# Three sixteen-head attentions: side products spread over the slots, the mask of z moved ahead of the next score, and the normalise step moved to GpSimd

## The chip, the cores and the metric

The program runs on one core of one Trainium2 chip. The metric is the device time of the whole program in microseconds (us), the median of the runs shown.

## The reference

The program is a four-layer decoder on eight sequences of 256 tokens of 128 features. Twelve sublayers are added to the tokens `x` one after another, each on a layer norm of `x`. Three of them are attentions with sixteen heads of eight features, and only these are touched here:

```python
x = x + _L1_xattn_ref(_layernorm(x), ctx, ...)        # causal, then a two-layer MLP
x = x + _L2_xattn_ref(ctx, ctx, _layernorm(x), mask)  # keys and values from ctx, a given 0/1 mask
x = x + _L3_attn_ref(_layernorm(x), ...)              # causal, low-rank ("latent") weights
```

Each computes, for every head, softmax(q k^T * scale, masked) v over the 256 tokens of a sequence. The other nine sublayers are the same before and after.

## The kernel before

All three attentions are one function, `attention16`. A **unit** is one of the eight sequences; a **pair** is two of its sixteen heads, so there are 8 pairs in a unit and 64 in an attention. Tokens lie on the partitions in two halves of 128. An fp32 number is split into three bf16 pieces (GpSimd, `split_in_three`), and DMAs stack the pieces so that the six products of pieces are one bf16 matmul over 64 rows; two heads of a pair take rows 0 to 63 and 64 to 127 of the array.

The work is ordered by hand in **slots**, one pair a slot. Every engine walks the same slots and runs what falls due in each; semaphores join the engines. Pair n is scored in slot n. Twelve slots later (`BEHIND` = 12, and `r` is the slot less 12) its products are made again, transposed and with the row maxima subtracted, into the one buffer `ps_z`. In TensorE's order a slot is: `shift(r)` (z = scores again, transposed), `score(slot)`, `hide(ps_z)` (a matmul that adds the mask to z), `hide(ps_s)` (the same for the scores), `turn_back`, the side products, `weigh` (probabilities times values). Then:

- ScalarE takes exp of `ps_z` (L1667) when the hide of z is done; the next `shift` waits for that exp.
- VectorE reduces the scores to row maxima (`take_maxima`, L1354 and L1355, in the masked attention L1357). `ps_s` has two buffers, so a score waits for the maxima of two slots before.
- In even slots TensorE weighs four heads into `ps_o` (L1540). ScalarE copies the sums (L1673); in odd slots TensorE turns them back (L1555) and VectorE divides (`divide`, L1378 and L1382). `ps_o` is one bank, so a `weigh` waits for the `divide` before it.
- The **side products** share one bank, `ps_p`, each waiting until the one before is read out: maxima transposed (L1548), tokens transposed (L1469), q (L1475), k (L1479), v (L1486), the mixed heads transposed (mix, L1562), and in the masked attention the output projection (y, L1570). `xn`, the normalised tokens, is one buffer made on VectorE for the next unit (`normalise_unit`, L1342).
- After the maxima, VectorE splits them in three pieces (`split_maxima`) and SyncE stores them as rows of `queries` (L1266); the first `shift` of the unit, four slots later, waits for these rows.

By slot number modulo 8 the side products before are: 0 maxima, 2 mix and tokens, 3 y and q, 4 k, 6 v. The first attention has no y in the slots (an MLP follows) and the latent one has neither mix nor y: it adds to `x` from `mixed` in position 3.

An attention begins with slots before pair 0, in which unit 0 and 1 are prepared. TensorE runs three 512-column filler matmuls (L54) in each negative slot, and twelve in slot 0. GpSimd sets up constants, splits q and k, turns the integer masks into bf16 (`make_masks`) and adds the output bias (`add_bias`).

## Time and profile before

| what | value |
|---|---|
| median of 3 runs | 1993.07 us (1988.14 to 1995.74) |
| span of the profiled execution | 1991.5 us |
| TensorE busy | 1615.1 us, 81% |
| VectorE busy | 1231.2 us, 62% |
| ScalarE busy | 823.4 us, 41% |
| GpSimd busy | 606.1 us, 30% |
| first, masked, latent attention: first shift to last shift | 112.6, 163.2, 111.0 us |

The span runs from the first to the last instruction of one profiled execution; it lies 1.6 us below the median. The profile gives no time of its own for that execution besides the span. In the tables PE is TensorE's matmuls, PEld its weight loads, DVE is VectorE, ACT ScalarE, POOL GpSimd. The profile leaves the digits off the tile names, so `x_` is the first as well as the masked attention, and `a_` is the latent one.

### The profile page before, as it was taken

The page shows a single profiled execution, that of the slowest core. Times are in us where ns is not written, and L with a number is a line of the kernel's source. Part 1 is how long each engine was busy: PE and PEld are TensorE (multiplying, and loading weights), DVE is VectorE, ACT ScalarE, POOL GpSimd, SP SyncE. Part 2 cuts the span into 40 slices and gives each one's busy share as a digit, 9 for nine tenths or more (in the row PEclk, how much of TensorE's full clock was granted, in tenths as well). Part 3 has the DMA queues.
Part 4 walks back from the last instruction along what each step waited for, and adds up shares of the span by engine and source line. Part 5 has one row for each costly group of instructions (what it writes and reads, how often), then busy time and mean ns, then how long its engine had stood idle before and what let it go on. Part 6 is the DMA issues. An engine that isn't in the chain of part 4 may idle for free. (4 is left out here: it accounts for less than half of the span.)

```text
span 1991.5 us, 34855 instructions
## 1 busy us (share of the span) xinstructions
PE 1615.1 (81%) x12400; PEld 1077.5 (54%) x12400; DVE 1231.2 (62%) x4249; ACT 823.4 (41%) x1760; POOL 606.1 (30%) x742
## 2 busy tenths in 40 slices
PE   3378767888779897757988799978877888999888
PEld 1146434454547787644444366745546654677556
DVE  6868645575378999533666333326848875899632
ACT  2232345366227786732344443314643410333422
POOL 4605122430024535304531000022202115777221
PEclk8677877999879999878999898889988987999999
DMA  2000001320036777613321000022210000000000
GB/s 86 0 12 1 10 30 50 83 60 14 7 128 213 262 248 262 219 37 116 84 58 38 18 1 0 1 61 65 62 61 3 1 0 1 2 2 3 2 0 22
DMA packets 81332, 115.59 MB, mean 58 GB/s; under 512 B 8464, under 2 KB 62608, under 8 KB 80400
## 3 DMA queue, kind: packets, MB, share of 16 engines
q0 software_dynamic: 18432, 67.38, 9.7%
q1 hardware_dynamic: 60144, 44.90, 8.1%
q8 instruction: 96, 1.57, 0.3%
q10 hardware_dynamic: 2592, 1.18, 0.3%
q14 instruction: 68, 0.56, 0.1%
HBM read 88.85 MB, written 1.05 MB: 45 GB/s over the span
## 5 line engine op out<-in xcount | busy, mean ns | idle before, releaser
L2643 POOL DMA_INDIRECT f_rows<-tree_table,f_index x128 | 128.8, 1006 | 185.8 <-DVE f_index L2704 75.7
L2844 PE MATMUL f_ps_y<-f_rows,shared_sb 128*128 128x128 f32 x1024 | 129.2, 289 | 31.3 <-ACT f_rows L2916 31.3
L2916 ACT ACTIVATE f_rows<-f_rows,f_low_act 128x128 f32<-128x128 f32 x512 | 153.0, 387 | 0.8
L1667 ACT ACTIVATE x_probs<-x_ps_z 128x768 f32<-128x768 f32 (+1 forms) x128 | 117.4, 917 | 85.6 <-PE x_ps_z L1527 57.6
L82 POOL TENSOR_TENSOR rstd<-moments,shared_sb 128x12 f32<-128x12 f32 (+3 forms) x22 | 4.6, 207 | 480.9 <-DVE moments L66 480.8
L2844 PEld LDWEIGHTS f_ps_y<-f_rows,shared_sb 128*128 128x128 f32 x1024 | 124.5, 203 | 37.2 <-ACT f_rows L2916 33.9
L2743 DVE CUSTOM_DVE_ANT_0 f_rows<-f_rows,f_xn 128x128 f32<-128x128 f32 x512 | 111.3, 287 | 24.2 <-DMA f_rows<-tree_table,f_index 24.2
L1357 DVE TENSOR_REDUCE x_minus_max<-x_ps_s 128x4 f32<-128x1024 f32 x64 | 77.8, 1223 | 73.7 <-PE x_ps_s L1527 73.5
L2095 PE MATMUL f_ps_h<-f_xnT,weights 128*128 128x512 f32 x144 | 76.7, 661 | 2.4 <-ACT f_hT L2160 2.1
L2160 ACT ACTIVATE f_hT<-f_ps_h,weights 128x512 f32<-128x512 f32 x72 | 48.6, 685 | 71.4 <-PE f_ps_h L2095 69.7
L2072 DVE SCALAR_TENSOR_TENSOR x_tokens<-f_ps_y,f_chosen,x_tokens 128x128 f32 (+1 forms) x128 | 36.0, 344 | 67.1 <-PE f_ps_y L2107 67.1
L2107 PEld LDWEIGHTS f_ps_y<-weights,f_hT 128*128 128x128 f32 x576 | 69.7, 192 | 14.3 <-issue 12.6
L3382 ACT ACTIVATE r_probs<-r_ps_z 128x768 f32<-128x768 f32 x64 | 51.9, 810 | 58.5 <-PE r_ps_z L3262 58.5
L2107 PE MATMUL f_ps_y<-weights,f_hT 128*128 128x128 f32 x576 | 73.2, 278 | 0.0
L1514 PE MATMUL x_ps_z<-x_queries,x_keys 64*128 64x256 bf16 (+1 forms) x512 | 46.8, 261 | 27.0 <-ACT x_probs L1667 25.8
L3064 POOL TENSOR_TENSOR r_q_swapped<-r_q_swapped,weights 128x256 f32<-128x256 f32 x64 | 58.4, 912 | 31.4 <-DVE r_q_swapped L3118 30.8
L1540 PE MATMUL x_ps_o<-x_probs,x_v_ones 128*32 128x256 f32 (+1 forms) x1024 | 61.7, 358 | 2.0 <-DVE x_mixed L1382 1.2
L1667 ACT ACTIVATE a_probs<-a_ps_z 128x768 f32<-128x768 f32 x64 | 51.8, 810 | 27.3 <-PE a_ps_z L1523 27.2
L3262 PE MATMUL r_ps_z<-r_queries,r_keys 64*128 64x256 f32 (+1 forms) x512 | 59.1, 350 | 2.8 <-ACT r_probs L3382 2.7
L3250 PE MATMUL r_ps_s<-r_keys,r_queries 64*128 64x128 f32 (+1 forms) x512 | 54.0, 329 | 4.1 <-DVE r_minus_max L3127 2.6
L2836 PE MATMUL f_ps_y<-weights,f_maskedT 128*128 128x128 f32 (+2 forms) x384 | 54.2, 292 | 3.3 <-ACT f_maskedT L2903 3.3
L3262 PEld LDWEIGHTS r_ps_z<-r_queries,r_keys 64*128 64x128 f32 x512 | 44.1, 186 | 21.8 <-issue 14.1
(661 smaller groups left out, 4191.6 us busy)
## 6 DMA issues: line engine op xcount, KB each, us to landing
x_queries<-x_pieces SPq DMA_DIRECT2D x96, 64.0 KB, 2.1
x_keys<-x_pieces SPq DMA_DIRECT2D x84, 64.0 KB, 2.1
a_queries<-a_pieces SPq DMA_DIRECT2D x48, 64.0 KB, 2.1
weights<-w_L_ffn SPq DMA_DIRECT2D x1, 2953.5 KB, 9.9
a_keys<-a_pieces SPq DMA_DIRECT2D x42, 64.0 KB, 2.1
weights<-w_L_ffn SPq DMA_DIRECT2D x1, 2449.0 KB, 9.7
weights<-w_L_ffn SPq DMA_DIRECT2D x1, 2176.0 KB, 9.2
f_rows<-tree_table,f_index POOLq DMA_INDIRECT x128, 6.1
```

The lines of the kernel that those rows point to most:

```text
L1357: last = v.tensor_reduce(peaks.rearrange("p j h -> p h j"), scores.rearrange("p h (j k) -> p h j k", j=HALVES), AX.X, ALU.max, negate=True)
L1540: last = pe.matmul(out[V1 * i:V1 * (i + 1), a:T], v_ones[:, u % KEPT, half, SIDE * group + i, :], probs[:, r % HELD, i % 2, at:at + T - a] ...
L1667: a.activation(probs[:, r % HELD, :, :], ps_z[:, :, 0:WIDE], ACT.Exp, scale=scale).then_inc(exped, 1)
L2095: pe.matmul(ps_h[:, i % 2, :], w["up"][:, i * P:(i + 1) * P], xnT[:, :], start=True, stop=True).then_inc(up_made, 1)
L2107: last = pe.matmul(out, hT[:, i % 4, j * P:(j + 1) * P], w["down"][:, i * P:(i + 1) * P], start=c == 0, stop=c == CH - 1 and e < E)
L2643: pool.indirect_dma_start(rows[:, place(u, j), tree, :], None, g.tree_table, bass.IndirectOffsetOnAxis(index[:, u % 2, low, j * TREES + tr ...
L2743: last = v.tensor_tensor_reduce(row, row, xn[:, u % KEPT, j, :], 1.0, 0.0, ALU.mult, ALU.add, low_act[:, u % 3, j * TREES + tree, f:f + 1])
L2836: last = pe.matmul(ps_y[:, u % SUMS, j, :], maskedT[0:k, i, :], w["out"][0:k, i * P:(i + 1) * P], start=j == 0 and i == 0, stop=False)
L2844: last = pe.matmul(ps_y[:, u % SUMS, j, :], g.ident, rows[:, place(u, j), tree, OUT + f * D:OUT + (f + 1) * D], start=False, stop=(low, j, ...
L2916: last = a.activation(row, row, ACT.Copy, scale=low_act[:, u % 3, j * TREES + tree, f:f + 1])
L3064: step(pool.tensor_tensor(part, part, w["sin_q"], ALU.mult))
L3262: last = pe.matmul(ps_z[:, i, out], keys[rows, u % RINGS, k:k + P], queries[rows, u % RINGS, p, q:T], start=q == 0, stop=q > 0)
```

## The change

Three edits, all in `attention16`:

1. The slots of the side products move. By slot number modulo 8 they are afterwards: 0 maxima, 1 y, 2 tokens, 3 q, 4 mix, 5 k, 7 v; position 6 has none. The latent attention's add moves from position 3 to 4. The normalise step of a unit moves from 15 to 18 slots ahead of its first score, and with it the load of the masks on SyncE's queue. The slots now begin three earlier, at -18 for -15, and end two later.
2. On TensorE the hide of z stands directly behind `shift`, ahead of the next `score`.
3. All units but the first are normalised on GpSimd instead of VectorE. In GpSimd's order the step comes ahead of the slot's bias, splits and masks.

```diff
--- before.py
+++ after.py
@@ -1160,7 +1160,7 @@
     GROUPS = NH // SIDE
     LAG = 4
     BEHIND = PAIRS + LAG
-    FIRST, LAST = -PAIRS - 7, ALL + BEHIND + PAIRS + 4
+    FIRST, LAST = -PAIRS - 10, ALL + BEHIND + PAIRS + 6
     RINGS, HELD, KEPT = 4, 4, 4
     STACK_DMAS = 2 * len(PRODUCTS) + 1
     SEEN = ((slice(0, P), slice(STACK, P)), (slice(0, STACK), slice(0, P)))
@@ -1209,12 +1209,12 @@
 
         unit_at = lambda n: n // PAIRS if n % PAIRS == 0 and 0 <= n < ALL else None
         pair_at = lambda n: n if 0 <= n < ALL else None
-        norm_in, tokens_in, q_in, k_in, v_in = (lambda slot, early=e: unit_at(slot + early) for e in (15, 14, 13, 12, 10))
+        norm_in, tokens_in, q_in, k_in, v_in = (lambda slot, early=e: unit_at(slot + early) for e in (18, 14, 13, 11, 9))
         queries_out, keys_out = (lambda slot, early=e: unit_at(slot + early) for e in (11, 8))
         maxima_in = lambda slot: unit_at(slot - PAIRS)
         group_in = lambda r, late: (r - late) // 2 if r % 2 == late % 2 and 0 <= (r - late) // 2 < ALL // 2 else None
         weighed_in, sums_in, back_in = (lambda r, late=n: group_in(r, late) for n in (2, 3, 5))
-        mix_in, y_in = (lambda r, late=n: unit_at(r - late) for n in (14, 15))
+        mix_in, y_in = (lambda r, late=n: unit_at(r - late) for n in (16, 21 if tail else 16))
         slots = range(FIRST, LAST)
 
         side_taken = {"maxima": maxima_taken, "mix": mix_taken, "y": y_taken, "tokens": tokens_taken, "q": q_taken, "k": k_taken, "v": v_taken}
@@ -1320,7 +1320,17 @@
                 pool.tensor_tensor(g.x[:, of, :], g.x[:, of, :], w["out_b"].rearrange("p (o d) -> p o d", o=1).broadcast_to([P, HALVES, D]),
                                    ALU.add).then_inc(bias_added, 1)
 
+            def normalise_unit(u):
+                pool.wait_ge(xT_made, u)
+                for half in range(HALVES):
+                    n = u * HALVES + half
+                    last = pool.tensor_scalar(xn[:, half, :], g.x[:, n, :], g.moments[:, n, 0:1], g.rstd[:, n:n + 1],
+                                              ALU.subtract, ALU.mult)
+                last.then_inc(xn_ready, 1)
+
             for slot in slots:
+                if norm_in(slot) is not None and norm_in(slot) > 0:
+                    normalise_unit(norm_in(slot))
                 if tail and v_in(slot - 1) is not None:
                     add_bias(v_in(slot - 1))
                 if q_in(slot) is not None:
@@ -1335,11 +1345,9 @@
         def _(v):
             step = Chain(v, steps)
 
-            def normalise_unit(u):
-                v.wait_ge(xT_made, u)
+            def normalise_first():
                 for half in range(HALVES):
-                    n = u * HALVES + half
-                    last = v.tensor_scalar(xn[:, half, :], g.x[:, n, :], g.moments[:, n, 0:1], g.rstd[:, n:n + 1],
+                    last = v.tensor_scalar(xn[:, half, :], g.x[:, half, :], g.moments[:, half, 0:1], g.rstd[:, half:half + 1],
                                            ALU.subtract, ALU.mult)
                 last.then_inc(xn_ready, 1)
 
@@ -1402,7 +1410,7 @@
                     last = v.bn_stats(g.x_stats[:, n, :], g.x[:, n, :])
                 last.then_inc(stats_taken, 1)
 
-            normalise_unit(0)
+            normalise_first()
             v.wait_ge(g.loaded[name], 16)
             if causal:
                 by_half = lambda m: w[m].rearrange("p (i k) -> p i k", i=2)
@@ -1415,8 +1423,6 @@
             v.memset(v_ones[:, :, :, :, :], 1.0).then_inc(ones_ready, 1)
             for slot in slots:
                 r = slot - BEHIND
-                if norm_in(slot) is not None and norm_in(slot) > 0:
-                    normalise_unit(norm_in(slot))
                 if pair_at(slot) is not None:
                     take_maxima(slot)
                 if maxima_in(slot) is not None:
@@ -1581,12 +1587,11 @@
                     fill_wait(pe, g, ps_z[:, 0, :], 512, 5)
                 if pair_at(r) is not None:
                     shift(r)
+                    hide(ps_z, r // PAIRS, 1).then_inc(shifted, 1)
                 if pair_at(slot) is not None:
                     score(slot)
                 if not causal and unit_at(slot) is not None:
                     pe.wait_ge(mask_ready, unit_at(slot) + 1)
-                if pair_at(r) is not None:
-                    hide(ps_z, r // PAIRS, 1).then_inc(shifted, 1)
                 if pair_at(slot) is not None:
                     hide(ps_s[:, slot % 2, :, :], slot // PAIRS, 0).then_inc(scored, 1)
                 if back_in(r) is not None:
```

## Rows read from the trace of the kernel before

**Rows 1.** Windows view, masked attention, slots 12 to 75 (busy us by engine)
```profile
962.80:1126.00 163.20, 141.85 (x1345) 69.11 (x1345) 91.06 (x174) 84.19 (x118) 42.11 (x49) 1.00 0.18 46
```

**Rows 2.** Timeline, latent attention, slots 53 to 55 (start, duration, engine, line)
```profile
1441.82 0.34 PE L1514 MATMUL a_ps_z<-a_queries,a_keys 64*128 64x256 bf16 x4
...
1442.70 0.43 DVE L1354 TENSOR_REDUCE a_minus_max<-a_ps_s 128x2 f32<-128x256 f32 x1
...
1443.40 0.34 PE L1514 MATMUL a_ps_z<-a_queries,a_keys 64*128 64x256 bf16 x4 [0.38 <-ACT a_probs L1667]
...
1444.16 0.59 PEld L1540 LDWEIGHTS a_ps_o<-a_probs,a_v_ones 128*32 128x32 f32 x16 [0.16 <-DVE a_mixed L1382]
...
1444.97 0.34 PE L1514 MATMUL a_ps_z<-a_queries,a_keys 64*128 64x256 bf16 x4
```

**Rows 3.** Timeline, first attention: starts of slots 32, 33, 35, 36 and 40
```profile
417.62 0.34 PE L1514 MATMUL x_ps_z<-x_queries,x_keys 64*128 64x256 bf16 x4 [0.37 <-ACT x_probs L1667]
...
419.49 0.34 PE L1514 MATMUL x_ps_z<-x_queries,x_keys 64*128 64x256 bf16 x4
...
424.16 0.34 PE L1514 MATMUL x_ps_z<-x_queries,x_keys 64*128 64x256 bf16 x4
...
425.83 0.34 PE L1514 MATMUL x_ps_z<-x_queries,x_keys 64*128 64x256 bf16 x4
...
433.36 0.34 PE L1514 MATMUL x_ps_z<-x_queries,x_keys 64*128 64x256 bf16 x4 [0.38 <-ACT x_probs L1667]
```

**Rows 4.** Timeline, latent attention: starts of slots 40, 48, 52 and 56
```profile
1417.73 0.34 PE L1514 MATMUL a_ps_z<-a_queries,a_keys 64*128 64x256 bf16 x4 [0.37 <-ACT a_probs L1667]
...
1433.01 0.34 PE L1514 MATMUL a_ps_z<-a_queries,a_keys 64*128 64x256 bf16 x4 [0.37 <-ACT a_probs L1667]
...
1440.25 0.34 PE L1514 MATMUL a_ps_z<-a_queries,a_keys 64*128 64x256 bf16 x4 [0.46 <-ACT a_probs L1667]
...
1446.55 0.34 PE L1514 MATMUL a_ps_z<-a_queries,a_keys 64*128 64x256 bf16 x4 [0.37 <-ACT a_probs L1667]
```

**Rows 5.** Timeline, masked attention: starts of slots 32, 40, 51, 52 and 53
```profile
1016.61 0.39 PE L1514 MATMUL x_ps_z<-x_queries,x_keys 64*128 64x256 bf16 x4 [0.47 <-ACT x_probs L1667]
...
1040.32 0.39 PE L1514 MATMUL x_ps_z<-x_queries,x_keys 64*128 64x256 bf16 x4 [0.47 <-ACT x_probs L1667]
...
1071.74 0.39 PE L1514 MATMUL x_ps_z<-x_queries,x_keys 64*128 64x256 bf16 x4
...
1074.09 0.40 PE L1514 MATMUL x_ps_z<-x_queries,x_keys 64*128 64x256 bf16 x4
...
1076.61 0.39 PE L1514 MATMUL x_ps_z<-x_queries,x_keys 64*128 64x256 bf16 x4
```

**Rows 6.** Timeline, masked attention: an exp after the last score
```profile
1124.87 1.02 ACT L1667 ACTIVATE x_probs<-x_ps_z 128x1024 f32<-128x1024 f32 x1 [1.02 <-PE x_ps_z L1527]
```

**Rows 7.** Timeline, masked attention: matmuls that change the row count on TensorE
```profile
952.64 1.24 PE L54 MATMUL x_ps_z<-filler 128*128 128x512 bf16 x5
...
953.81 0.39 PE L1502 MATMUL x_ps_s<-x_keys,x_queries 64*128 64x256 bf16 x4
...
1098.74 0.38 PE L1502 MATMUL x_ps_s<-x_keys,x_queries 64*128 64x256 bf16 x4
...
1099.05 0.61 PE L1527 MATMUL x_ps_z<-x_masks,x_ident 128*128 128x512 bf16 x2
```

**Rows 8.** Timeline, latent attention: its first fillers and first token transposes
```profile
1323.94 2.72 PE L54 MATMUL a_ps_s<-filler 128*128 128x512 bf16 x6 [1.06 <-PEq L1735]
...
1326.45 0.64 PE L1469 MATMUL a_ps_p<-shared_sb,a_xn 128*128 128x128 f32 x2
```

**Rows 9.** Timeline (first row) and views of lines L92 and L3053 (ns min/median/max)
```profile
1405.80 0.58 DVE L1342 TENSOR_SCALAR a_xn<-x_tokens,moments,rstd 128x128 f32<-128x128 f32 x2
...
L92 POOL TENSOR_SCALAR a_xn<-x_tokens,moments,rstd x12: 784/2026/2768, 25.7 to 74.6; 128x128 f32<-128x128 f32 x12
...
L3053 POOL TENSOR_SCALAR f_hid<-x_tokens,moments,rstd x16: 787/794/1299, 1680.1 to 1844.2; 128x128 f32<-128x128 f32 x16
```

## The prediction

> **What bounds the kernel now.** I read the windows view first, for the slots in which both halves of the pipeline run, then the timeline slot by slot. In the masked attention TensorE is busy 141.85 of 163.20 us at full clock, VectorE 91 and GpSimd 42 [rows 1]. TensorE is near its limit, yet not at it, so a slot's length has to be read. A slot is the distance from one `shift` (L1514) to the next. "Position" below is the slot number modulo 8.
>
> The light slots of the causal attentions (no side product) show two chains of the same length. Slot 53 starts at 1441.82 and slot 54 at 1443.40, which waited 0.38 us for the exp: 1.58 us for shift, score, hide of z and exp. But the pair of slots ends only at 1444.97, and there the other chain ends too: scores hidden, reduce at 1442.70, divide, and `weigh` at 1444.16, which had waited 0.16 us for VectorE's `mixed`; the next shift follows 0.81 us later [rows 2]. So an odd and an even slot together take 3.15 us by VectorE's chain alone. An earlier exp cannot shorten that.
>
> A full unit (eight slots with all sides) takes 433.36 - 417.62 = 15.74 us in the first attention [rows 3], 1433.01 - 1417.73 = 15.28 us in the latent one, and a light unit 13.54 us. In the light unit positions 0 to 3 take 1440.25 - 1433.01 = 7.24 us and positions 4 to 7 take 6.30 us [rows 4]. The first four hold the split of the maxima on VectorE and the rows that its DMAs store. In the masked attention a full unit takes 23.71 us [rows 5].
>
> **Edit 1 and 3, causal attentions.** Positions 0 to 3: VectorE's chain and the stored rows gave 7.24 us in the light unit, where nothing was normalised and only maxima stood beside. With the normalise gone from VectorE (0.58 us, two instructions [rows 9]) and mix gone from position 2, a full unit should come down to the same 7.24 us: tokens hide under the wait of `weigh`. Positions 4 to 7: an even slot with two transposes takes 419.49 - 417.62 = 1.87 us, an odd slot with q takes 425.83 - 424.16 = 1.67 us [rows 3]; a plain even slot takes 1.57 us [rows 2]. So the first attention gets 1.87 (mix) + 1.67 (k) + 1.57 + 1.67 (v) = 6.78, a unit of 14.02 us, 1.72 less. In the latent one position 4 is plain, but the add now stands on VectorE between the maxima of positions 4 and 5, where it was behind the divide. The light slots show 3.24 us in place of 3.15 where the add is near [rows 4]; here I charge 0.4 us, for the add and statistics less VectorE's idle time: 1.57 + 1.67 + 1.88 + 1.67 = 6.79, a unit of 14.03 us, 1.25 less. There are three full units in each (slots 24 to 47). The unit before them, without mix or add, saves 1.56, and slots 12 to 15 about 0.9 (k and v leave slots that weigh or start to). The two light units lose a little: mix stands in the open now, +0.13 each in the first, and the late add costs +0.23 each in the latent one. Sum: first 3 x 1.72 + 1.56 + 0.9 - 0.26 = 7.4 us, latent 3 x 1.25 + 1.56 + 0.9 - 0.46 = 5.8 us.
>
> In slots 0 to 11 no exp runs and VectorE's reductions set the pace, so each normalise that leaves it (0.58 us, twice) shortens them by something between nothing and itself: 0.8 us in each causal attention, 1.3 in the masked one (its scores are longer and one of its two normalises runs beside a busy GpSimd). Together 2.9.
>
> **Edit 2.** In the causal attentions every matmul of shift, score and hide uses 64 rows, so the exchange costs TensorE nothing. It brings the exp forward by the time of a score, and [rows 2] say that this is worth nothing in a light pair. I take 0; the bound on the other side is half of the exp wait of 0.38 us in some 20 odd slots of each, 7 us in both.
>
> In the masked attention the hides use all 128 rows and the score 64. Before, a slot had the order 64, 64, 128, 128; afterwards 64, 128, 64, 128: two more changes. A score's four matmuls of 256 columns, two at a time, are issued in 0.21 us, but the hide follows 0.31 us after its start; and behind five fillers (5 x 0.21 us = 1.05, a filler being half of the 0.42 us that it takes at half clock [rows 8]) the 64-row score starts after 1.17 us [rows 7]. So each change costs about 0.10 us, and each slot that TensorE bounds gets 0.20 us longer. The exp alone would allow 2.04 us a slot (1.02 idle and 1.02 of its own, with no score between [rows 6]).
>
> The Trainium skill, "TensorEngine Tiling (Array Packing)", Key Properties, says that a change of tiling mode, not just of tile, drains TensorE. By that rule this edit has a price; the trace agrees with a gap at each change. A full drain read as the 0.19 us by which five modelled fillers outlast their issue (1.24 for 1.05) would make the slot 0.38 longer rather than 0.20, 8 us more in all.
>
> With 0.20 the slots of the masked attention are: even plain 2.52 + 0.20 = 2.72; even with two transposes 2.93 (0.21 more, my estimate, between 0 and the 0.30 of [rows 3]); odd with y, q, k or v 2.35 + 0.20 = 2.55; odd plain 2.1, an estimate at which TensorE's own work and the exp come out alike [rows 5, 6]. A full unit is 3 x 2.93 + 2.72 + 4 x 2.55 = 21.7 us. The waits of position 2 (tokens for mix) and 3 (q for VectorE's add) are gone, since each side's reader has a slot's time. That saves 2.0 us in each of two full units and 2.3 in the third before y begins. The first unit loses 0.5, the two light ones 0.45 each (four even slots and y pay 0.20, three plain odd ones win 0.18), slots 12 to 15 win 0.45. Sum: 5.4 us.
>
> **The three early slots.** Each attention begins 9 fillers later: its six took 1326.45 - 1323.94 = 2.51 us at half clock before the first transposes [rows 8], so nine are 3.8 us, and 1.9 at full clock. TensorE has nothing else to do then, and everything behind waits: q, its split, the keys' DMAs on ScalarE's queue. Part comes back because the clock has risen by the time the projections run, where it was at half in part, and because the first split no longer runs beside VectorE's long memset. I take 1.8, 2.2 and 1.2 us, 5.2 in all; bounds 0 and 11.4.
>
> **GpSimd.** A normalise is two tensor_scalar of 128x128. GpSimd shows 0.79 us in the median for this form in one stage and 2.03 (0.78 to 2.77) in another, beside heavy VectorE work [rows 9]. At 0.79 a unit costs 1.6 us, at 2.77 5.5. It falls due at position 6 and is needed by the tokens at position 2, four slots on, never under 5.6 us; GpSimd is three quarters idle [rows 1]. I take 0: the cover is that idle time; without it one late unit costs up to 4 us. The masks load earlier on SyncE and are needed 18 slots on: 0. The last unit's output in the masked attention has one add more in line ahead of mix: +1, by judgment, since y of the unit before now comes after the last divide.
>
> **Sum.** -7.4 - 5.8 - 5.4 - 2.9 + 5.2 + 1.0 = -15.3, say -15. The span of 1991.5 becomes 1976.5; it stands 1.6 under the median, so the median of 1993.07 becomes 1978.
>
> **The rivals.**
> - *The exchange is worth its face.* Row changes cost nothing under the longer streams, and the causal light pairs do shorten. The masked attention then gains 9 us more (about 45 slots x 0.20) and the causal ones up to 7. For it: exp waits stand in front of nearly every odd slot's end. Against it: the gaps of [rows 7] and the 0.16 us of [rows 2]. Time: 1978 - 9 - 3 (half of the 7) = 1966. Chance 0.14.
> - *Given back.* The waits move instead of going: the longer lead-in costs its 3.8 us in full three times (+6), and tokens or k meet a late GpSimd or a late reader in the full units (+0.5 us in ten units). Time: 1978 + 11 = 1989, not to be told from no change. For it: one shared bank and one `xn` leave every side behind the one before. Against it: the slack that the spread leaves by [rows 3 to 5]. Chance 0.29.
> - *Slower: the row changes cost more than they did*, because the hide of z and the weight loads of the score can't overlap and the weight queue runs dry. Place: the masked attention's 52 scoring slots. Each slot would need 0.7 us for two changes in place of 0.20 to make the whole slower by 0.5% (15 + 10 = 25 us over 52 slots, 0.5 each). At 0.8 the time is 1978 + 31 = 2009. For it: it is the one edit with a price in every slot. Against it: the two changes that are read cost 0.10 to 0.12 each [rows 7]. Chance 0.07.
> - The forecast itself: 0.50.
>
> **Chances and range.** One can tell from no change only what is over about 0.5%, 10 us. Faster 0.50 + 0.14, of which a little falls inside 10 us: 0.62. Same: 0.31. Slower: 0.07. The range reaches down to the first rival and up to the second, 1965 to 1989; the forecast's own is 1970 to 1986.
>
> **What would show it.** Windows over the three stretches should be 105, 158 and 105 us from first to last shift. A full unit should be 14.0, 21.7 and 14.0 us. No tokens or q wait for ScalarE's mixT or VectorE's add. The masked attention's slots should show the hide 0.31 us behind the shift and the score 0.3 behind the last hide's issue. Light causal units should not be shorter. POOL's new rows should be near 0.8 us each, with tokens never waiting on them past slot 0. The first score of each attention should come 1 to 2.5 us later than before, counted from its first filler. The forecast is wrong if light pairs shorten (chain misread), if tokens wait on GpSimd, or if a masked slot grows by other than 0.2.

## The result and the profile after

The changed kernel takes 1959.87 us (median of 4 runs, 1956.94 to 1962.79) against 1990.69 us for the kernel before (4 runs): ratio 0.984, 95% interval 0.982 to 0.986. The forecast was 1978 with a range of 1965 to 1989; it has the right sign, the gain is twice what it said, and the time lies below the range. A second measurement of the same kernel later gave 1962.60 against 1989.99 us, ratio 0.986 (0.984 to 0.988).

The table splits the span of each profile at the same events: the first filler of an attention, its first score, the first and the last shift (slots 12 and 75), and the first instructions of the stages between. The starts are read to 0.1 us, that of the last shift at its fourth matmul, so these stretches are 0.1 us longer than the distance from shift to shift ([rows 1] and the windows below). "Untouched" is all the rest, whose code is the same in both kernels (but for the last slots of the first attention, which are counted there).

| us | before | after | change | forecast |
|---|---|---|---|---|
| first filler to first score, three attentions | 23.6, 23.4, 24.8 | 23.1, 23.7, 22.9 | -2.1 | +5.2 |
| slots 0 to 11 | 16.2, 20.0, 16.2 | 16.5, 19.1, 15.9 | -0.9 | -2.9 |
| slots 12 to 75, first attention | 112.7 | 103.8 | -8.9 | -7.4 |
| slots 12 to 75, masked | 163.3 | 155.7 | -7.6 | -5.4 |
| slots 12 to 75, latent | 111.1 | 104.2 | -6.9 | -5.8 |
| tails of masked and latent | 13.4, 10.0 | 14.9, 10.4 | +1.9 | +1.0 |
| sum | 534.7 | 510.2 | -24.5 | -15.3 |
| untouched | 1456.8 | 1444.8 | -12.0 | 0 |

The windows view of the changed kernel over slots 12 to 75 of the first, the masked and the latent attention, the middle one answering to [rows 1] (columns: stretch, length, busy us and count of PE, PEld, DVE, ACT, POOL, then granted clock, DMA share, GB/s):

```profile
375.20:478.90 103.70, 94.48 (x1549) 59.45 (x1550) 72.45 (x190) 71.80 (x118) 30.62 (x52) 1.00 0.20 48
943.40:1099.00 155.60, 146.88 (x1320) 59.54 (x1344) 89.38 (x166) 85.94 (x118) 48.60 (x57) 1.00 0.18 45
1337.20:1441.30 104.10, 92.58 (x1535) 58.18 (x1534) 77.44 (x218) 70.38 (x113) 27.50 (x47) 1.00 0.20 47
```

In the masked attention TensorE's busy time rose from 141.85 to 146.88 us while the stretch shrank by 7.6: it now leaves 9 us idle. The rise belongs to the exchange: the changed kernel without it (an experiment below) is busy for 137.94 us of 151.30. The timeline of the masked attention's slot 54 and the start of slot 55 shows where it comes in (start, duration, engine, line; rows of VectorE and most weight loads are left out, here and in the timelines below):

```profile
1051.17 0.39 PE L1520 MATMUL x_ps_z<-x_queries,x_keys 64*128 64x256 bf16 x4
1051.49 0.60 PE L1533 MATMUL x_ps_z<-x_masks,x_ident 128*128 128x512 bf16 x2
1052.03 0.12 PEld L1508 LDWEIGHTS x_ps_s<-x_keys,x_queries 64*128 64x128 bf16 x4 [0.42 <-issue]
1052.03 0.39 PE L1508 MATMUL x_ps_s<-x_keys,x_queries 64*128 64x256 bf16 x4
1052.14 1.02 ACT L1672 ACTIVATE x_probs<-x_ps_z 128x1024 f32<-128x1024 f32 x1 [1.02 <-PE x_ps_z L1533]
...
1052.36 0.60 PE L1533 MATMUL x_ps_s<-x_masks,x_ident 128*128 128x512 bf16 x2
1052.89 1.07 PE L1546 MATMUL x_ps_o<-x_probs,x_v_ones 128*32 128x256 f32 x16
...
1053.90 0.39 PE L1520 MATMUL x_ps_z<-x_queries,x_keys 64*128 64x256 bf16 x4
```

A shift or score is issued in 0.21 us and two hides in 0.42. Start to start here: shift to hide 0.32, hide to score 0.54, score to hide 0.33, hide to `weigh` 0.53: every one is 0.11 to 0.12 us longer than its issue. The score's first weight load starts together with its first matmul here; in slot 53 of the kernel before, where the score follows a shift of the same tile, it started 0.11 us ahead of it (1076.73 for 1076.84). Whether the price of a change is a drain of the array or this load that nothing hides, no run separates. The exp starts 0.97 us after the shift, where it started 1.2 us after it. The slot is 2.73 us.

The starts of the first attention's slots 33, 34, 35 and 41 in the timeline, to be set beside [rows 3]:

```profile
410.02 0.34 PE L1520 MATMUL x_ps_z<-x_queries,x_keys 64*128 64x256 bf16 x4
...
411.43 0.34 PE L1520 MATMUL x_ps_z<-x_queries,x_keys 64*128 64x256 bf16 x4 [0.21 <-ACT x_probs L1672]
...
413.73 0.34 PE L1520 MATMUL x_ps_z<-x_queries,x_keys 64*128 64x256 bf16 x4
...
423.80 0.34 PE L1520 MATMUL x_ps_z<-x_queries,x_keys 64*128 64x256 bf16 x4
```

A full unit, here from slot 33 to slot 41, is 13.78 us (15.74 before, 14.02 forecast). GpSimd's normalise, in the view of its line:

```profile
L1327 POOL TENSOR_SCALAR x_xn<-x_tokens,moments,rstd x28: 783/792/806, 347.4 to 1013.6; 128x128 f32<-128x128 f32 x28
L1327 POOL TENSOR_SCALAR a_xn<-x_tokens,moments,rstd x14: 790/792/804, 1310.1 to 1384.3; 128x128 f32<-128x128 f32 x14
...
  PE x_ps_p L1475: 3.2, 2
  PE a_ps_p L1475: 1.6, 1
```

It is 0.79 us each time, as assumed, and TensorE's tokens waited for it three times, once in each lead-in.

### The profile page after: what moved, and what is told of

Same layout as the page of the kernel before. It is cut to its first block and busy times, and to the rows that moved or that the text cites. A ratio compares the mean times of both kernels' runs of the same rounds, so it can differ in the third digit from the quotient of the medians.

```text
span 1955.0 us, 34849 instructions
## 1 busy us (share of the span) xinstructions
PE 1599.1 (82%) x12367; PEld 1058.0 (54%) x12427; DVE 1219.7 (62%) x4207; ACT 824.3 (42%) x1760; POOL 638.0 (33%) x784
## 5 line engine op out<-in xcount | busy, mean ns | idle before, releaser
L2165 ACT ACTIVATE f_hT<-f_ps_h,weights 128x512 f32<-128x512 f32 x72 | 48.6, 685 | 71.8 <-PE f_ps_h L2100 70.0
L1672 ACT ACTIVATE a_probs<-a_ps_z 128x768 f32<-128x768 f32 x64 | 51.9, 810 | 13.4 <-PE a_ps_z L1529 12.4
```

The costliest lines, as they stand in the source:

```text
L1672: a.activation(probs[:, r % HELD, :, :], ps_z[:, :, 0:WIDE], ACT.Exp, scale=scale).then_inc(exped, 1)
```

## The experiments

All times are of slots 12 to 75 unless another stretch is named, in the order first, masked, latent; before they are 112.7, 163.3, 111.1 and after 103.8, 155.7, 104.2 us. Whole-kernel ratios are to the kernel before, with their 95% intervals. Within one kernel a given slot repeats to 0.01 or 0.02 us from unit to unit, and slots 12 to 75 repeat to 0.4 us from one profile to the next, which is why most verdicts rest on slots and not on medians. Stretches outside them do not repeat so well.

### The kernel before once more

> The kernel before once more, with nothing changed. It measures what a comparison here can tell and how much a stage that no edit touches differs from one execution to the next. In the traces of before and after the untouched stages together differ by about 11 us (4.7 us ahead of the first attention, 4.0 in the trees, 2.5 in the block behind the latent attention), the touched ones by about 24. Theory A (scatter): the ratio is 1.000 within 0.3%, and the first filler of the first attention starts between 335 and 340 us, the stage from 534.2 to 919.4 lasts 381 to 386 us. Theory B (the untouched stages are shorter in the changed kernel for a reason of the change, such as the place of its code): the untouched stages repeat the times of before within 1 us in all, 339.9 us and 385.2 us.

Ratio 0.9996 (0.9979 to 1.0013); the 19 runs of before in this batch lay between 1987.3 and 2000.1 us. Slots 12 to 75: 112.7, 163.3, 111.5. The stretch before the first attention took 338.9 us and the trees (a long untouched stage between the first attention and the masked one) 382.9, for 339.9 and 385.2: scatter, as the first theory had it. First filler to first score, the **lead-in** from here on, took 24.5, 23.0, 23.4, so a single lead-in differs by up to 1.4 us in the same kernel (and by 3.7 in the changed kernel's repetition below).

### Edit 1 alone: side products in slots of their own

```diff
-  FIRST, LAST = -PAIRS - 7, ALL + BEHIND + PAIRS + 4
+  FIRST, LAST = -PAIRS - 7, ALL + BEHIND + PAIRS + 6
...
-  norm_in, tokens_in, q_in, k_in, v_in = (... (15, 14, 13, 12, 10))
+  norm_in, tokens_in, q_in, k_in, v_in = (... (15, 14, 13, 11, 9))
...
-  mix_in, y_in = (... (14, 15))
+  mix_in, y_in = (... (16, 21 if tail else 16))
```

> Edit 1 alone: side products in slots of their own, the normalise step still on VectorE 15 slots ahead, hide of z behind the score, no early slots. Forecast on record: it is this edit that gains; the masked attention without the price of the row changes gets some 14 us shorter from slot 12 to 75 (5.4 + 9), the first 7, the latent 5.5: about -26 us in all, a full masked unit 20.9 to 21.0 us. Rival (the exchange carries part of the gain and costs TensorE nothing): masked -6 to -8, first and latent -6 and -4, about -17 in all, a full masked unit 21.5 us or more.

Ratio 0.988 (0.985 to 0.990). Slots: 107.5, 151.6, 107.6, so -5.2, -11.7, -3.5. A full masked unit is 19.86 to 20.41 us. The spread is the largest gain, and nearest to the forecast (-7, -14, -5.5) in the masked attention. In full units of the causal ones position 2 takes 2.64 us (before: 3.10 in the first, 2.64 in the latent), because VectorE's normalise still holds its place there: with the normalise on GpSimd and all else alike it is 2.13 (the changed kernel without edit 2, below).

### Edit 2 alone: hide of z behind the shift

```diff
     if pair_at(r) is not None:
         shift(r)
+        hide(ps_z, r // PAIRS, 1).then_inc(shifted, 1)
     if pair_at(slot) is not None:
         score(slot)
...
-    if pair_at(r) is not None:
-        hide(ps_z, r // PAIRS, 1).then_inc(shifted, 1)
```

> Edit 2 alone: the hide of z directly behind the shift in all three attentions. Forecast on record: nothing in the causal attentions (light unit 13.54 us), and 0.20 us more in each TensorE-bound slot of the masked one, about 45 of them: +9 us in all. Rival (worth its face): the causal attentions lose their waits for the exp, 0.38 us in 20 odd slots each, -7 us together, and the masked one pays 0.20 in even slots only and wins it back in odd ones: 0 to -3; total -7 to -10.

Ratio 0.996 (0.994 to 0.998). Slots: 109.1, 164.5, 108.8, so -3.6, +1.2, -2.3. In the causal attentions the odd slots of positions 1, 5 and 7 fall from 1.58 to 1.41 us and position 3 with q from 1.67 to 1.57; the even ones with k or v stay at 2.18 to 2.20, and a light unit falls from 13.54 to 13.22 in the first attention and to 13.31 in the latent one. In the masked attention an even slot goes from 2.52 to 2.73 and an odd one from 2.26 to 2.05. The forecast that [rows 2] make the exp worthless is refuted: the exp bounded the odd slots, and with its wait cut from 0.38 to 0.21 us the first attention's light pairs of positions 4 to 7 take 3.03 and 3.11 us, not 3.15.

### Edit 3 alone: normalise on GpSimd

```diff
-  FIRST, LAST = -PAIRS - 7, ...
+  FIRST, LAST = -PAIRS - 10, ...
...
-  norm_in, ... (15, 14, 13, 12, 10)     # called on VectorE
+  norm_in, ... (18, 14, 13, 12, 10)     # called on GpSimd, unit 0 on VectorE
```

> Edit 3 alone: all units but the first normalised on GpSimd, 18 slots ahead, three early slots with nine more fillers, sides and hides as before. Forecast on record: lead-ins +5.2 us together, slots 0 to 11 -2.9, and in full units VectorE is relieved of 1.16 us at a place where the tokens, not VectorE, are late (mix in the same slot), so 0 to -0.5 a unit, -4 at most: total -2 to +2. Rival (the lead-in costs nothing, because the nine fillers lift the clock before the projections): lead-ins 0 to -1, total -3 to -6.

Ratio 0.993 (0.990 to 0.995). Slots: 112.3, 163.4, 109.2. Where tokens do not share their slot with mix, position 2 falls from 2.64 to 2.13 us; where they do (first and masked, full units) nothing moves. Slots 0 to 11 take 16.2, 19.0, 15.6, and the lead-ins 23.2, 23.8, 23.5. The touched stretches give -5.0 us, where -2 to +2 had been expected and -3 to -6 by the rival; the ratio's interval begins at -9. The rest of it is not in them (the untouched code took 1449.4 us in this profile, 7.4 less than in that of the kernel before), and it is not explained by this run.

### Nine more fillers and nothing else

```diff
-  FIRST, LAST = -PAIRS - 7, ...
+  FIRST, LAST = -PAIRS - 10, ...
```

> The kernel before with three empty slots more at the start of each attention, so nine more fillers of 512 columns and nothing else. It prices the lead-in. Forecast on record: +1.9 to +3.8 us a lead-in less what the risen clock gives back, 1.2 to 2.2 each, +5.2 in all. Rival (TensorE has slack in the lead-in: before, it sat idle 3.86 us there until ScalarE had copied the second unit's tokens): the first filler to the first score lasts 23 to 24.5 us as before in each, 0 in all.

Ratio 1.000 (0.998 to 1.002). Lead-ins 24.7, 25.4, 25.3 us: 3.6 us more than before in all, 4.5 more than in its repetition. So the fillers alone cost a good part of the 5.2 us forecast, and in the changed kernel something gives it back. Against edit 3 alone, which has the same fillers, the lead-ins are 1.5, 1.6 and 1.8 us longer. The timeline of the first attention's second unit says where. First the kernel before, then edit 3 alone; the bracket is TensorE's idle time and what ended it:

```profile
355.39 1.19 PE L1475 MATMUL x_ps_p<-x_xnT,weights 128*128 128x256 f32 x2 [3.86 <-ACT x_xnT L1645]
```

```profile
349.39 0.41 PE L1475 MATMUL x_ps_p<-shared_sb,x_xn 128*128 128x128 f32 x2 [1.44 <-POOL x_xn L1327]
...
352.25 0.67 PE L1481 MATMUL x_ps_p<-x_xnT,weights 128*128 128x256 f32 x2 [1.81 <-ACT x_xnT L1651]
...
353.49 0.70 PE L1485 MATMUL x_ps_p<-x_xnT,weights 128*128 128x256 f32 x2
```

Before, TensorE had run out of fillers and stood still for 3.86 us in one piece, until ScalarE had issued the first unit's key DMAs and copied the second unit's tokens; behind it q took 1.19 us and k 0.98, near twice their 0.67 and 0.59 us at full clock. With fillers alone the gap is 3.45 us and k takes 1.06 behind it. With the normalise on GpSimd the tokens come later, the gap falls in two parts of 1.44 and 1.81 us, and q and k take 0.67 and 0.70 at full clock. The changed kernel has 1.61 and 1.81 us there, and the same 0.67. The mean granted clock of that lead-in is 0.82 before, 0.86 with fillers alone and 0.92 with edit 3 alone and in the changed kernel. Behind the gap of 3.86 us the granted clock was 0.50 (1.2 GHz), behind the split one 1.00 (2.4 GHz).

### The changed kernel without edit 2

```diff
     if pair_at(r) is not None:
         shift(r)
-        hide(ps_z, r // PAIRS, 1).then_inc(shifted, 1)
     if pair_at(slot) is not None:
         score(slot)
...
+    if pair_at(r) is not None:
+        hide(ps_z, r // PAIRS, 1).then_inc(shifted, 1)
```

> The changed kernel with edit 2 undone in all three attentions. From the runs of single edits (slots 12 to 75, change against before in us): sides -5.2, -11.7, -3.5; exchange -3.6, +1.2, -2.3; GpSimd -0.4, +0.1, -1.9; all three together -8.9, -7.6, -6.9. New theory: the exchange is worth what the exp-bound slots can give. In the causal attentions odd slots go from 1.58 to 1.41 us while they carry no side, and are 1.57 either way with one; in the masked one odd slots go from 2.26 to 2.05 without a side but are 2.38 for 2.26 with one, and even slots pay 0.21. So without the exchange slots 12 to 75 should last about 105.5, 150.7 and 105.7 us (after: 103.8, 155.7, 104.2), -1.8 in all against the changed kernel. Rival (gains add up): 107.4, 154.5, 106.5, +4.7.

Ratio 0.987 (0.983 to 0.991). Slots: 105.4, 151.3, 105.3. So inside the changed kernel edit 2 is worth -1.6, +4.4, -1.1: together it costs 1.7 us, where alone it gained 4.7. The timeline of slot 45 of the masked attention (odd, with k) in the kernel without edit 2 shows why:

```profile
1031.11 0.39 PE L1520 MATMUL x_ps_z<-x_queries,x_keys 64*128 64x256 bf16 x4
...
1031.34 0.38 PE L1508 MATMUL x_ps_s<-x_keys,x_queries 64*128 64x256 bf16 x4
1031.65 0.60 PE L1533 MATMUL x_ps_z<-x_masks,x_ident 128*128 128x512 bf16 x2
...
1032.30 1.02 ACT L1673 ACTIVATE x_probs<-x_ps_z 128x1024 f32<-128x1024 f32 x1 [0.67 <-PE x_ps_z L1533]
1032.53 0.38 PE L1561 MATMUL x_ps_o<-shared_sb,x_sumsT 128*128 128x128 f32 x2
...
1032.75 0.60 PE L1485 MATMUL x_ps_p<-ctx_features,weights 128*128 128x256 f32 x2
1033.37 0.39 PE L1520 MATMUL x_ps_z<-x_queries,x_keys 64*128 64x256 bf16 x4
```

The exp ends at 1033.32 and k at 1033.35: the slot of 2.26 us is full on both sides. Bringing the exp forward then gives nothing, and two more changes make it 2.38. In the kernel before, k and v stood in even slots and the exp alone bounded every odd slot but position 3 of the full units.

### Edit 2 in the causal attentions only

```diff
+    if pair_at(r) is not None and causal:
         hide(ps_z, r // PAIRS, 1).then_inc(shifted, 1)
...
+    if pair_at(r) is not None and not causal:
+        hide(ps_z, r // PAIRS, 1).then_inc(shifted, 1)
```

> The changed kernel with edit 2 undone in the masked attention alone. New theory: 103.8, 150.7 and 104.2 us from slot 12 to 75, 5 us less than the changed kernel, a full masked unit 19.9 us for 21.1. Rival (the exchange alone cost the masked attention 1.2 us, and that is what it costs here): 1.2 us less, 154.5 us.

Ratio 0.987 (0.984 to 0.990), median 1963.80. Slots: 103.8, 151.3, 104.2: the masked stage is 4.4 us shorter than in the changed kernel, as expected, while the median shows none of it. Its other stages took 1452.5 us.

### The changed kernel without edit 3

```diff
-  FIRST, LAST = -PAIRS - 10, ...
+  FIRST, LAST = -PAIRS - 7, ...
...
-  norm_in, ... (18, 14, 13, 11, 9)      # called on GpSimd
+  norm_in, ... (15, 14, 13, 11, 9)      # called on VectorE
```

> Edits 1 and 2 without edit 3: normalise on VectorE 15 slots ahead, no early slots. If VectorE's normalise stands in the way of the tokens once mix has left their slot, position 2 is 2.8 us for 2.29 in four units of each causal attention: slots 12 to 75 last 105.9, 156.7 and 106.3 us, +5 in all against the changed kernel. Rival (GpSimd is worth only what it was alone, 0.4 and 1.9): 104.2, 155.6, 106.1, +2.2. Either way the lead-ins are within 1 us of 23.6.

Ratio 0.989 (0.987 to 0.992). Slots: 105.9, 156.0, 106.0. Edit 3 is worth 2.1 and 1.8 us in the causal attentions (position 2: 2.80 against 2.30), five times what it was worth alone in the first, and 0.3 in the masked one. The lead-ins are 24.5, 23.1 and 24.2 us, 71.8 in all as in the kernel before.

### The changed kernel once more

> The changed kernel once more. The stages that no edit touches took 1444.8 us in its first profile, and between 1449.4 and 1465.6 us in nine other kernels with the same code there, at granted clocks that differ. Theory A (the first profile met a high clock in them; the change itself is worth the 24.5 us of the touched stages): the touched stages repeat within 1 us (slots 12 to 75 103.8, 155.7, 104.2 us), the untouched ones take 1450 us or more, and the ratio is nearer 0.987 than 0.984. Theory B (the change shortens the untouched stages too): they take 1447 us or less again and the ratio is 0.984 or lower.

Theory A holds for the slots (103.8, 155.7, 104.2), the untouched stages (1453.7 us) and the ratio (0.986). It does not hold for the lead-ins: they took 23.0, 23.1 and 26.6 us, so the touched stretches are 22.1 us shorter than before in this profile, not 24.5. The latent lead-in has the same two gaps as the first profile, but the granted clock fell in it and q took 1.19 us. Here is q's timeline row, then the windows of the latent lead-in in the first profile and in this one:

```profile
1317.78 1.19 PE L1481 MATMUL a_ps_p<-a_xnT,a_w_q 128*128 128x256 f32 x2 [1.74 <-ACT a_xnT L1650]
...
1298.40:1321.20 22.80, 19.37 (x84) 9.48 (x84) 5.15 (x8) 3.42 (x8) 11.68 (x22) 0.92 0.51 140
...
1300.50:1327.10 26.60, 23.18 (x86) 10.87 (x88) 5.11 (x7) 3.43 (x8) 12.58 (x23) 0.77 0.49 131
```

Over all fourteen profiles the untouched code took 1444.8 to 1465.6 us. The windows view shows what goes with it, first the stretch before the first attention and that behind the latent one in the changed kernel's first profile, then the same two stretches of the kernel of the next experiment, whose untouched code took 1465.1 us:

```profile
0.00:335.60 335.60, 204.07 (x942) 126.22 (x952) 223.06 (x524) 115.91 (x196) 109.91 (x109) 0.77 0.06 20
...
1451.80:1955.00 503.20, 435.88 (x3278) 306.21 (x3294) 342.94 (x1085) 152.60 (x342) 198.95 (x254) 0.93 0.03 10
```

```profile
0.00:343.70 343.70, 212.87 (x943) 136.05 (x953) 223.18 (x524) 116.00 (x196) 109.93 (x109) 0.75 0.06 20
...
1460.90:1970.00 509.10, 440.78 (x3278) 308.12 (x3294) 343.73 (x1085) 152.75 (x342) 198.41 (x254) 0.92 0.03 9
```

VectorE, ScalarE and GpSimd are busy for the same time within 0.5%; TensorE alone is busy for longer, 8.8 and 4.9 us, at a mean granted clock of 0.75 for 0.77, and 0.92 for 0.93.

### Three repairs, the first on the number of changes

```diff
+    if not causal:          # in score(r), ahead of its matmuls
+        for i in range(2):
+            pe.matmul(ps_s[...], ident16, masks[...], start=True, stop=False)
...
-  mix_in, y_in = (... (16, 21 if tail else 16))
+  mix_in, y_in = (... (16, 21 if tail else 15))
-    if slot < 0:
+    if -PAIRS - 7 <= slot < 0:
         fill_wait(pe, g, ps_s[:, 0, 0, :], 512, 3)
```

> The changed kernel with three repairs, in stages that do not touch each other. (a) Masked attention: on TensorE shift, hide of z, hide of s, score, so the exp stays early and the row count changes twice a slot instead of four times. New theory (each change costs 0.10 us): even slots go back from 2.72 to 2.52 and 2.94 to 2.73, odd slots stay at 2.05 without a side and take 2.20 with one; slots 12 to 75 last 143 to 146 us for 155.7. Rival (it is the hide of z between shift and score that costs, not the number of changes): 155 us as now, or 151 as without the exchange. (b) Latent attention: the add one slot earlier, behind the maxima of position 3; position 6 goes from 2.07 to 1.55 us in full units and from 2.00 to 1.70 in light ones, slots 12 to 75 last 102 us for 104.2. (c) No fillers in the three early slots: the first filler to the first score 22 us for 23.1, 23.7, 22.9 if the fillers delay the first tokens and the clock rises anyway, no less if the clock then falls in the wait for the second unit.

Ratio 0.986 (0.984 to 0.988). Slots: 103.8, 155.7, 102.9. (b) held in direction: -1.3 us, position 6 at 1.79 us for 2.07. Position 6 had been expected at 1.55, and the stretch at 102. (c) held: lead-ins 22.4, 22.8, 22.0, 2.5 us less in all than in the changed kernel's first profile, although the granted clock fell in each. The next two kernels drop the fillers too, and there it is 1.9 and 0.6 less. (a) failed as forecast: even slots 2.62 plain, 2.99 with tokens or mix, odd slots with a side 2.42, where 2.52, 2.73 and 2.20 had been expected. My count had left out two places: hide or score to `weigh` is a change as well (128 to 32 columns), and a score that stands last needs one more before the turn back. Counted so, a plain even slot has three changes from shift to weigh (after: four; before: two), and the three lengths 2.62, 2.73, 2.52 differ by 0.10 a change.

### Score at the end of the slot

```diff
     shift(r)
     hide(ps_z, ...)
-    score(slot)             # masks first, then scores
+    mask_scores(slot)       # the masks alone, start=True
     turn_back, side products, weigh
+    score(slot)             # masked attention only
```

> As the last kernel, but in the masked attention the score stands at the end of TensorE's slot, directly ahead of the next shift; hide of s still directly behind hide of z. Read from the starts in the run before: every change of the matmul's tile costs 0.10 to 0.12 us over the issue of 0.21 us, that between hide or score and weigh (128x128 or 64x128 to 128x32) as well, so moving the score behind the hides had not taken two changes away: four of them stand in an odd slot and in one with transposes, three in a plain even one (2.42, 2.99, 2.62 us measured). New theory (0.10 for each change, wherever it stands): now score and next shift share a tile, one change fewer in plain even slots and two fewer in the others: even plain 2.52, even with two transposes 2.73 to 2.79, odd with a side 2.20, odd plain 2.04 by the exp; slots 12 to 75 last 146 to 148 us (changed kernel 155.7, without the exchange 151.3). Rival (what costs is that the hide of z stands directly behind the shift, not the changes): even slots stay at 2.62 and 2.99, 155 us. The other stages as in the run before: 103.8 and 102.9 us, first filler to first shift 38.3, 41.8 and 37.9 us. The ratio: 9 us less than the changed kernel in the masked attention and some 5 in the rest, 0.979 to 0.984.

Ratio 0.989 (0.986 to 0.992). Slots: 103.9, 162.4, 103.0. The forecast of 146 to 148 us failed. Odd slots with a side came down to 2.17 us, but `weigh` now waits for VectorE, as in slot 36:

```profile
1013.14 1.07 PE L1559 MATMUL x_ps_o<-x_probs,x_v_ones 128*32 128x256 f32 x16 [0.29 <-DVE x_mixed L1390]
```

### VectorE's maxima at the end of its slot, too

```diff
-    if pair_at(slot) is not None:
+    if causal and pair_at(slot) is not None:
         take_maxima(slot)
     ...  # split, divide, add
+    if not causal and pair_at(slot) is not None:
+        take_maxima(slot)
```

> As the last kernel, with VectorE's order changed to match in the masked attention: split, divide and add ahead of the slot's maxima. The last kernel bore out the price of the changes on TensorE (odd slots with a side 2.17 us for 2.42, and 2.80 for 2.99 in the even one with mix once its wait is taken off), but lost more: the score now ends the slot, its maxima start behind it, and the divide stood behind them, so each weigh waited 0.29 to 0.90 us for VectorE's mixed, y 0.68 us for the split, tokens 0.83 us for the add. Theory: these waits go. Even plain 2.52, even with tokens or mix 2.80, with maxima 2.75 to 2.95 (it needs the maxima of the last score, which end 1.4 us after that slot), odd with a side 2.17, odd plain 2.04; slots 12 to 75 last 147 to 149 us, against 155.7 in the changed kernel and 151.3 without the exchange. Rival (the maxima, 1.23 us of each slot, are late whatever the order, because they cannot start before the slot's end): weigh still waits and the stage lasts 155 us or more.

Median 1955.78 us (5 runs) against 1991.32, ratio 0.982 (0.979 to 0.984). Slots: 103.9, 148.9, 102.8: the shortest masked attention of all, 14.4 us under before. Slot 54 in the timeline, beside that of the changed kernel above:

```profile
1048.87 0.39 PE L1535 MATMUL x_ps_z<-x_queries,x_keys 64*128 64x256 bf16 x4
1049.19 0.61 PE L1548 MATMUL x_ps_z<-x_masks,x_ident 128*128 128x512 bf16 x2
1049.63 0.59 PE L1523 MATMUL x_ps_s<-x_masks,x_ident 128*128 128x512 bf16 x2
1049.83 1.02 ACT L1687 ACTIVATE x_probs<-x_ps_z 128x1024 f32<-128x1024 f32 x1 [1.02 <-PE x_ps_z L1548]
1050.16 1.07 PE L1561 MATMUL x_ps_o<-x_probs,x_v_ones 128*32 128x256 f32 x16
1051.16 0.39 PE L1510 MATMUL x_ps_s<-x_keys,x_queries 64*128 64x256 bf16 x4
...
1051.39 0.38 PE L1535 MATMUL x_ps_z<-x_queries,x_keys 64*128 64x256 bf16 x4
```

Two changes fewer, 2.52 us for 2.73, and the exp starts just as early after the shift. Score and next shift follow each other in 0.23 us. Even slots with mix are 2.73, odd ones with a side 2.17, odd plain ones 2.04. Only position 0 pays, 3.12 us for 2.94, since it waits 0.23 us for the maxima of the score just ahead. The forecast of 147 to 149 us held.

## Why the prediction was wrong

What failed most is the term for the three early slots: nine fillers, with "everything behind waits", were to cost 5.2 us, and the lead-ins came out 2.1 us shorter (0.9 longer in the second profile). Next to it stand the step that called the earlier exp worthless in light pairs, and the price of 2.55 us for an odd masked slot with a side. The gains of edit 1 and of the normalise were forecast well, and no rival of the three describes the outcome. The first one, the exchange worth its face, is nearest in time (1966) but its mechanism is half wrong: the exchange costs time in the changed kernel. Step by step:

- **Sides and normalise in the causal attentions: right.** -7.4 and -5.8 us had been forecast with nothing for the exchange; the changed kernel without the exchange shows -7.3 and -5.8, full units of 13.90 and 13.93 us (14.02 and 14.03) and 7.24 us in positions 0 to 3 (7.24). In this the near-exact sums are in part luck, since small errors cancel: odd slots with k or v are 1.58 us, not 1.67, and the light units of the first attention lost 0.36 us each instead of 0.13. The 1.67 was read in position 3, which takes 1.67 us in light units too, where the first attention has no side in it; nor is the 3.24 us of positions 3 and 4 the add's doing, as the first attention has the same without an add. The add is charged at 0.4 us but stands in the sum at 0.31 (1.88 for 1.57); it measured 0.38 without the exchange and 0.50 in the changed kernel.
- **"An earlier exp cannot shorten that": wrong.** The step took VectorE's 3.15 us for the pair's limit, but both chains ended together in [rows 2]: the exp of slot 54 ends at 1444.92 us, 0.05 us ahead of the next shift, as the row that stands between them shows.

```profile
1444.11 0.81 ACT L1667 ACTIVATE a_probs<-a_ps_z 128x768 f32<-128x768 f32 x1 [0.77 <-PE a_ps_z L1523]
```

  Moved alone, the exp gives 0.32 us a light unit in the first attention, and 0.17 us in positions 1, 5 and 7 and 0.10 in position 3 of a full one. In the changed kernel that is -1.6 and -1.1 us.
- **Row changes at 0.10 each: right.** The even slots grew by 0.21, from 2.52 to 2.73 and from 2.73 to 2.94, where 0.20 had been forecast for each. The Trainium skill, "TensorEngine Tiling (Array Packing)", Key Properties, says that a change of tiling mode drains TensorE. In kind the traces agree: every change has a price, here 0.10 to 0.12 us. The prediction's reading of a drain as 0.19 us each would have made these slots 2.90 and 3.11, and that is refuted. **"Odd with y, q, k or v 2.35 + 0.20 = 2.55": the term that was mis-sized.** It measured 2.38. The 2.35 was read in slot 51, position 3; other odd slots were at 2.26. Both stood there because of the exp, not of TensorE's work, so two changes on TensorE took the place of a wait. In slots 16 to 47 fourteen odd slots hold a side (y only from slot 33 on), which makes 14 x 0.17 = 2.4 us, about the 2.2 by which the masked stage beat the forecast. What else differs nearly cancels (slots 64 to 75, for which nothing was charged, take 0.34 us more).
- **The lead-ins: the largest error.** +5.2 forecast, -2.1 measured (and +0.9 in the second profile, whose latent lead-in took 26.6 us). The fillers alone cost 3.6 to 4.5 us, not far from it. The step "everything behind waits" overlooked the 3.86 us for which TensorE stood still ahead of the second unit, and what went with it on the clock. Edit 3 breaks that wait in two and took 1.5 to 1.8 us back in each attention. All 42 lead-ins of the fourteen profiles, by what stood in them:

| second unit normalised on | nine fillers more | TensorE's idle time, us | clock fell in or behind it | mean lead-in, us |
|---|---|---|---|---|
| VectorE | no | one gap, 3.2 to 4.6 | 15 of 15 | 23.9 |
| VectorE | yes | one gap, 3.3 to 3.5 | 3 of 3 | 25.1 |
| GpSimd | yes | two gaps, 1.4 to 1.6 and 1.7 to 1.8 | 1 of 15 | 23.5 |
| GpSimd | no | two gaps, 1.4 to 1.6 and 1.7 to 1.8 | 8 of 9 | 22.7 |

  "Fell" means from a granted clock of 1.00 to 0.50 before the first score. So neither the fillers nor the split of the gap held the clock by itself; both together did in all lead-ins but one. Even so the extra fillers did not pay: the shortest lead-ins have none, and a clock that falls. Over its five profiles edit 3 changes the three lead-ins by -1.3 us on average, so the forecast of +5.2 is wrong however the single ones scatter.
- **Slots 0 to 11**: -2.9 forecast, -0.9 measured; the net of it in the masked attention. **Tail**: +1.0 forecast, +1.9 and +1.1. **GpSimd**: 0 forecast for what its idle time covers, and nothing waited on it in the slots; in each lead-in the second unit's tokens waited 1.6 us.
- **The untouched stages: not a step of it at all, and 12.0 us of the first profile's 36.5.** The second profile has -3.1 us there. The touched stretches alone, 22.1 to 24.5 us shorter, would have left the time near the lower end of the range; the medians fell by 27.4 to 30.8 us, 3 to 9 more. Fourteen profiles show that the same code varies by 20.8 us, and two of them that TensorE's busy time and granted clock go with it; a share of the change in it is neither shown nor excluded, and the cause of these 3 to 9 us stays open.

Of the 9.2 us by which the touched stretches of the first profile beat the forecast, 7.3 are the lead-ins (4.3 of 6.8 in the second), 2.6 the causal slots (nearly all of it the exchange), 2.2 the masked ones; slots 0 to 11 and the tails take 2.9 back.

## What to carry to other kernels

When two chains end together, the row shows that neither is slack, not that one of them is the limit: price each by the work that it holds alone before calling an edit worthless, and ask again once another edit has filled the same slot (the exchange gained 4.7 us alone and cost 1.7 us beside the others). On TensorE, order work so that matmuls of one tile stand side by side across the slot's border, and give every engine that reads the moved result the same order; the first without the second cost 6.7 us more than the changed kernel, both together saved 6.8. And compare stages between events of the kernel rather than whole spans when the rest of the program varies by 20 us.

## What the runs showed of the hardware

A change of the matmul's tile cost 0.10 to 0.12 us over the issue of the matmul ahead, the same for 64 to 128 rows, for 128 to 64, and for 128 to 32 columns at `weigh` (1052.36 to 1052.89 for an issue of 0.42). It adds up only where TensorE bounds the slot: plain odd slots, bounded by the exp, are 2.04 us with four changes in the changed kernel and with two in the last one. In the first attention's lead-in TensorE ran at a granted clock of 0.50 (1.2 GHz) behind one idle gap of 3.86 us (q 1.19 us instead of 0.67) and at 1.00 (2.4 GHz) behind gaps of 1.44 and 1.81 us with fillers between; but behind gaps of 1.62 and 1.74 us the clock fell in one lead-in of the repeated changed kernel, and in eight of nine without the extra fillers. GpSimd's normalise was 0.79 us in all 42 instances, against a median of 2.03 for the same form in another stage [rows 9].
